# Three opening rounds of a fused Perceiver block re-made: earlier weight loads, Hadamard mean and absolute sums in round 0, ternary compares in round 1

## The reference

```python
# 1: cross attention, 16 heads, latent widths 64 (queries) and 32 (context)
C_q = Q @ Wq_d; C_kv = K @ Wkv_d
CqWqk = (C_q @ W_qk).reshape(b, n, H, LKV)
scores = einsum('bnhl,bkl->bhnk', CqWqk, C_kv) / sqrt(LKV)
out = einsum('bhnk,bkhd->bnhd', softmax(scores), (C_kv @ Wv_u).reshape(b, nkv, H, HD))
# 2: self attention, one head of width 128
q, k, v = split(x @ Wqkv + bqkv)
out = softmax(q @ k.T / sqrt(d)) @ v @ Wo + bo
# 3: feed forward with 4-bit activations and ternary weights
xh = x @ hadamard
scale = clip(max(abs(xh), axis=-1), 1e-5) / 7.0
xq = clip(round(xh / scale), -8, 7) * scale
wscale = clip(mean(abs(w), axis=1), 1e-5)
wq = where(w / wscale > 0.5, 1, where(w / wscale < -0.5, -1, 0)) * wscale
out = einsum('bsd,od->bso', xq, wq)
```

## Time and profile before

| | before |
|---|---|
| median of 3 runs (323.95 to 1033.37) | 324.0 us |
| profiled execution, its own time | 324.15 us |
| its span, first to last instruction | 322.4 us |
| PE busy (matmuls) | 310.4 us, 96% |
| DVE / ACT / POOL busy | 244.9 (76%) / 209.5 (65%) / 88.4 us (27%) |
| chain that ended last, by engine | PE 77%, DVE 10%, ACT 7% |
| DMA, mean over the span | 78 GB/s |

### The profile page before, as it was taken

How to read it: one execution, slowest core, us unless ns; L and a number is a source line. 1 busy time by engine, 2 the same in 40 slices (tenths; PEclk the granted TensorE clock), 3 DMA queues, 4 the chain that set the end, 5 groups by cost and what they waited for, 6 DMA issues and landing times.

```text
span 322.4 us, 8517 instructions
## 1 busy us (share of the span) xinstructions
PE 310.4 (96%) x3172; PEld 219.1 (68%) x3172; DVE 244.9 (76%) x524; ACT 209.5 (65%) x590; POOL 88.4 (27%) x129
## 2 busy tenths in 40 slices
PE   7987999999999999999999999999999999999995
PEld 6875776768576866667576867666675867675754
DVE  1499558887889878887889778987888877986435
ACT  1395867768596777767686777766776869582310
POOL 2000544041223324140323224240414123232320
PEclk9999999999999999999999999999999999999999
DMA  7891402050301403050302302050401010000000
GB/s 205 299 380 63 166 3 98 2 165 32 108 27 38 161 2 130 0 193 2 130 0 89 107 33 98 0 195 0 130 3 68 0 68 2 33 3 33 0 35 33
DMA packets 13481, 25.25 MB, mean 78 GB/s; under 512 B 3216, under 2 KB 3984, under 8 KB 13456
## 3 DMA queue, kind: packets, MB, share of 16 engines
q1 hardware_dynamic: 13456, 24.91, 22.4%
HBM read 20.71 MB, written 4.19 MB: 77 GB/s over the span
## 4 chain that ended last, share of the span: by engine, by line
PE 77%; DVE 10%; ACT 7%; issue 2%; DMA 1%; SPq 0%; POOL 0%; DVEq 0%
PE ps L691 12%; PE ps L729 8%; PE ps L638 7%; PE ps L806 6%; PE ps L786 5%; PE ps L648 4%; PE ps L829 4%; PE ps L838 4%; ACT prob L320 4%; PE ps L733 4%; DVE mx L450 3%; PE ps L709 2%; PE ps L741 2%; PE ps L669 2%; PE ps L812 2%
## 5 line engine op out<-in xcount | busy, mean ns | idle before, releaser
L320 ACT ACTIVATE prob<-ps,nmx,qk_scale 128x128 f32<-128x128 f32 x256 | 96.1, 468 | 40.5 <-DVE nmx L454 40.5
L691 PE MATMUL ps<-had_s,x3t 128*128 128x512 f32 x128 | 59.0, 604 | 1.1 <-ACT x3t L314 0.8
L450 DVE TENSOR_REDUCE mx<-ps 128x8 f32<-128x1024 f32 x32 | 38.9, 1216 | 11.1 <-PE ps L806 11.1
L691 PEld LDWEIGHTS ps<-had_s,x3t 128*128 128x128 f32 x128 | 23.0, 189 | 30.2 <-issue 28.4
L459 DVE TENSOR_REDUCE sum_a<-prob 128x8 f32<-128x1024 f32 x32 | 38.1, 1210 | 2.6 <-ACT prob L320 2.6
L303 POOL TENSOR_TENSOR qk_scale<-aux,power 128x1 f32<-128x1 f32 x16 | 8.8, 548 | 103.9 <-DVE aux L540 103.9
L314 ACT ACTIVATE prob_t<-ps 128x512 f32<-128x512 f32 x64 | 35.2, 622 | 0.6
L638 PE MATMUL ps<-ident,prob 128*128 128x128 f32 x256 | 33.7, 275 | 0.6 <-ACT prob L320 0.6
L729 PE MATMUL ps<-x2t,wqkv_s 128*128 128x128 f32 x256 | 32.7, 281 | 0.6 <-ACT x2t L314 0.2
L307 POOL TENSOR_TENSOR res<-prod,x 128x512 f32<-128x512 f32 x15 | 19.1, 1272 | 47.1 <-DVE prod L573 47.1
L729 PEld LDWEIGHTS ps<-x2t,wqkv_s 128*128 128x128 f32 x256 | 29.8, 191 | 2.6 <-ACT x2t L314 1.8
(11 more groups left out here) (120 smaller groups left out, 552.7 us busy)
## 6 DMA issues: line engine op xcount, KB each, us to landing
ct<-ctx_cols SPq DMA_DIRECT2D x16, 512.0 KB, 4.6
xt<-x_cols SPq DMA_DIRECT2D x16, 256.0 KB, 2.7
xr<-x_rows SPq DMA_DIRECT2D x16, 256.0 KB, 4.3
y<-res SPq DMA_DIRECT2D x15, 256.0 KB, 2.0
w_rows<-weight SPq DMA_DIRECT2D x1, 1024.0 KB, 8.8
had_s<-hadamard SPq DMA_DIRECT2D x1, 1024.0 KB, 9.0
wqkv_s<-wqkv SPq DMA_DIRECT2D x1, 768.0 KB, 10.6
wqk<-w_qk SPq DMA_DIRECT2D x2, 128.0 KB, 4.5
```

The costliest lines, as they stand in the source:

```text
L320: last = nc.scalar.activation(prob[:, h, :], ps[:, h // 4, (h % 4) * P:(h % 4) * P + P], ACT.Exp, bias=nmx[:, h:h + 1], scale=qk_scale[:])
L450: V.tensor_reduce(mx[:, h], ps[:, 2 * half:2 * half + 2, :].rearrange("p r (c k) -> p (r c) k", c=EC), AX.X, ALU.max).then_inc(done["mx"], 1)
L691: mm = pe.matmul(ps[:, B4, :], x3t[:, c, :], had_s[:, c, :], start=(c == 0), stop=(c == EC - 1))
```

## The change

Nothing of the arithmetic changes but the way in which the widened scales are turned (as transposes instead of matmuls with the identity). The orders of rounds 0, 1 and 2 do:
- SP: `had_s`, `w_rows` and the rows of pair 1 are loaded right behind the second context, `wqkv_s` behind the context of pair 2.
- Round 0: the latents are copied before the exponentials, DVE takes over three copies from ACT (`q_t`, `ckv`, the first quarter of `prob_t`), PE forms the Hadamard mean in two halves in bank B3 between the transposes, the scores of pair 1 come ahead of the weighted sum. DVE sums the absolute weights in four instructions, and then takes both halves of the largest scores. Of 14 filler matmuls 4 are left.
- Round 1: POOL centres the Hadamard matrix first (after the first half of `nmx` of pair 1), PE transposes all probabilities at once and then x2, DVE makes `const_row` and three ternary chunks, PE transposes the first half of the ternary weights (now by output rows, two chunks), and the scale row comes last.
- Round 2: the fourth ternary chunk on DVE behind `amax`, the second half of the ternary transposes in bank 0 (PE) and its copy (ACT).

```diff
@@ -211,21 +211,21 @@
             load_rows(0, 0)
             load_queries(1, 1)
             load_context(1, 1)
+            sp.dma_start(had_s[:], hadamard.rearrange("(c p) n -> p c n", p=P)).then_inc(ld_w["had"], 16)
+            sp.dma_start(w_rows[:], weight.rearrange("(c p) n -> p c n", p=P)).then_inc(ld_w["w"], 16)
+            load_rows(1, 1)
             for s in range(3):
                 sp.dma_start(b_qkv[:, s:s + 1], bqkv.rearrange("(s p o) -> s p o", p=P, o=1)[s]).then_inc(ld_w["b"], 16)
             sp.dma_start(bo_row[:], bo.rearrange("(o n) -> o n", o=1).to_broadcast([P, E])).then_inc(ld_w["b"], 16)
-            sp.dma_start(w_rows[:], weight.rearrange("(c p) n -> p c n", p=P)).then_inc(ld_w["w"], 16)
             sp.dma_start(wo_s[:], wo).then_inc(ld_w["wo"], 16)
             sp.wait_ge(zero_wv, 1)
             for r in range(4):
                 sp.dma_start(wv_bd[32 * r:32 * r + 32, :, 32 * r:32 * r + 32],
                              wv_u.rearrange("l (c r d) -> l c r d", c=EC, r=4)[:, :, r, :]).then_inc(ld_w["wv"], 16)
-            load_rows(1, 1)
-            sp.dma_start(had_s[:], hadamard.rearrange("(c p) n -> p c n", p=P)).then_inc(ld_w["had"], 16)
-            sp.dma_start(wqkv_s[:], wqkv.rearrange("(c p) n -> p c n", p=P)).then_inc(ld_w["wqkv"], 16)
             sp.wait_ge(made["lat"], 1)
             load_queries(2, 0)
             load_context(2, 0)
+            sp.dma_start(wqkv_s[:], wqkv.rearrange("(c p) n -> p c n", p=P)).then_inc(ld_w["wqkv"], 16)
...
             def hadamard_centred():
                 pool.wait_ge(hmean_read, 1)
+                pool.wait_ge(done["nmx"], 3)
                 for c in range(EC):
                     nc.gpsimd.tensor_tensor(had_s[:, c], had_s[:, c], had_mean[:], ALU.subtract).then_inc(had_ready, 1)
 
             def body(i, k, par, front, cross, self_, quant):
+                if isinstance(i, int) and i == 1:
+                    hadamard_centred()
...
+                def latents():
+                    after(act, made["lat"], i + 1)
+                    cols = slice(0 if alone(i) or par == 1 else P, P + 2 * SKV)
+                    copy(lat[:, cols], ps[:, B2, cols]).then_inc(read["lat"], 1)
+
+                def x2_turned():
+                    after(act, made["x2t"], i - 1)
+                    copy(x2t[:], ps[:, B2, :].rearrange("p (c t) -> p c t", c=EC)).then_inc(read["x2t"], 1)
+
+                def ternary_copy(half, bank):
+                    act.wait_ge(ternt_made, half + 1)
+                    copy(tern_t[:, :, 2 * half * P:2 * (half + 1) * P],
+                         ps[:, bank, :].bitcast(BF16).rearrange("p (c o) -> p c o", c=EC)).then_inc(ternt_read, 1)
+
+                if isinstance(i, int) and i == 0:
+                    latents()
                 if cross:
                     after(act, done["nmx"], i * 2)
                     exps(0, 6)
@@ -339,23 +356,24 @@
...
+                if isinstance(i, int) and i == 1:
+                    x2_turned()
+                    pt_copy(2)
+                    pt_copy(3)
+                    act.wait_ge(made["qt"], 3)
+                    q_copy(0, 0)
...
+                if isinstance(i, int) and i == 0:
+                    act.wait_ge(hmean_made, 1)
+                    copy(had_mean[:], ps[:, B3, :]).then_inc(hmean_read, 1)
...
+            def weight_sizes():
                 dve.wait_ge(ld_w["w"], 16)
-                V.tensor_reduce(w_abs[:], w_rows[:], AX.X, ALU.add, apply_absolute_value=True).then_inc(wabs_done, 1)
-                dve.wait_ge(wabs_done, 1)
+                for c in range(EC):
...
+                if first and i == 0:
+                    dve.wait_ge(made["qt"], 2)
+                    V.tensor_copy(q_t[:, 1], ps[:, B2, :].rearrange("p (c b q) -> p b c q", c=EC, b=2)).then_inc(read["qt"], 1)
+                    dve.wait_ge(made["ckv"], 2)
+                    V.tensor_copy(ckv[:, 1], ps[:, B1, 0:2 * SKV]).then_inc(read["ckv"], 1)
+                    sums(0)
+                    dve.wait_ge(made["pt"], 1)
+                    V.tensor_copy(prob_t[:, 0, :, :], ps[:, 0, :].rearrange("p (c t) -> p c t", c=EC)).then_inc(read["pt"], 1)
                     dve.wait_ge(ld_w["b"], 64)
                     V.tensor_copy(bv_wide[:], b_qkv[:, 2:3].to_broadcast([P, P])).then_inc(bvw_done, 1)
-                    ternary()
-                    dve.wait_ge(cb_made, 1)
-                    V.tensor_tensor(const_row[:], ps[:, B4, :], bo_row[:], ALU.add).then_inc(const_ready, 1)
+                    row_variance()
+                    dve.wait_ge(done["exp"], 2)
+                    row_scale()
+                    sums(1)
+                    weight_sizes()
+                    weight_scales()
+                    dve.wait_ge(made["s"], 2)
+                    largest(1, 0)
+                    largest(1, 1)
+                if first and i == 1:
+                    output_bias()
+                    dve.wait_ge(done["rsum"], 1)
+                    sums(0)
+                    ternary(0)
+                    sums(1)
+                    second_query()
+                    ternary(1)
+                    row_variance()
+                    row_scale()
+                    second_max()
+                    ternary(2)
...
+                    if first and i == 2:
+                        ternary(3)
...
-                pe.wait_ge(hmean_read, 1)
+                pe.wait_ge(ternt_read, 1)
                 for o in range(EC):
-                    mm = pe.matmul(ps[:, B4, o * P:(o + 1) * P], w_wide[:, o, :], ident[:], start=True, stop=True)
+                    mm = pe.transpose(ps[:, B4, o * P:(o + 1) * P], w_wide[:, o, :], ident[:])
                 mm.then_inc(row_made, 1)
 
-            def hadamard_mean():
...
+                for c in range(c0, c1):
+                    mm = pe.matmul(ps[:, B3, :], mean_w[:], had_s[:, c, :], start=(c == 0), stop=(c == EC - 1))
+                if c1 == EC:
+                    mm.then_inc(hmean_made, 1)
+
+            def ternary_transposed(half, bank):
+                pe.wait_ge(tern_done, 2 * (half + 1))
+                pe.wait_ge(const_ready, 1)
                 for c in range(EC):
-                    mm = pe.matmul(ps[:, B4, :], mean_w[:], had_s[:, c, :], start=(c == 0), stop=(c == EC - 1))
-                mm.then_inc(hmean_made, 1)
-
-            def ternary_transposed(half, bank):
-                pe.wait_ge(tern_done, EC)
-                if half == 0:
-                    pe.wait_ge(const_ready, 1)
...
-                        keep_busy(10, B3)
+                        keep_busy(4, B4)
+                        after(pe, read["lat"], i + 1)
+                        projected()
+                        hadamard_mean(0, 2)
                     transposed(0)
                     transposed(1)
                 if first and i == 0:
-                    after(pe, read["lat"], i + 1)
-                    projected()
-                    wide_bias()
+                    hadamard_mean(2, EC)
+                if first and i == 1:
+                    transposed(2)
+                    transposed(3)
+                    x2_turned()
+                    paired_projection()
...
+                if first and i == 2:
+                    pe.wait_ge(read["pt"], i * 4 + 1)
+                    ternary_transposed(1, 0)
+                if cross and not (first and i == 1):
                     transposed(2)
                     transposed(3)
                 if first and i == 0:
-                    keep_busy(4, B3)
-                if first and i == 1:
-                    wide_scale()
+                    wide_bias()
                 if self_:
...
+                if first and i == 0:
+                    scores()
+                if cross:
+                    weighted_sum()
+                if first and i == 1:
+                    ternary_transposed(0, B4)
+                if self_:
+                    after(pe, done["exp2"], i - 1, 2)
+                    pe.transpose(ps[:, B3, 0:P], p2[:], ident[:]).then_inc(made["p2t"], 1)
+                if front and not (first and i == 0):
+                    scores()
                 if self_:
...
-                if first and i == 0:
-                    ternary_transposed(0, B4)
-                    ternary_transposed(1, B3)
+                if first and i == 1:
+                    wide_scale()
```

179 lines of the change are left out of this document (93 added, 86 removed).

## The result

| | before | after |
|---|---|---|
| median | 323.93 us (19 runs, 323.14 to 326.11) | 322.61 us (20 runs, 321.47 to 324.84) |
| profiled execution, its span | 322.4 us | 320.5 us |
| mean granted clock of the profiled execution | 0.999 | 0.993 |

The account below looks back on a forecast made before the run. The prediction took PE to bound the kernel, so gains in rounds 0 to 2 move the end equally. Its terms, -3.2 us up to round 2 and +0.6 us in round 2, gave -2.6 us: 321.4 us, range 320.5 to 323.0.

Parts of the forecast that it names:

- the likeliest case: Rounds 0 to 2: the reordering gains as summed, -2.6 us, for 321.0 to 321.9 us; chance 0.52.
- the second case: Contention or late wait: POOL and DVE lock-out in SBUF, or pair 3's queries 1 us late; 322.0 to 322.9 us, chance 0.22.
- All four signs of "wrong": Granted clock under 1.00 after 29; PE waiting on x2n; longer round-1 DVE/POOL rows; PE or DVE waiting on a load.
- The opening of round 1 and the exponentials: Round 1 opens at 26.3 instead of 28.83; exponentials of pair 1 start at 26.85, 3.3 us sooner.
- The new wait of 2.2 us ahead of the second transposes: Round 1: PE waits from 30.8 to 33.0 for the second half of the exponentials, where the Hadamard mean lay.
- -3.2 us up to round 2: Rounds 0 and 1: round 2 opens at 44.4 instead of 47.63, 3.2 us gained.
- +0.6 us in round 2: Round 2: 8 ternary transposes on PE (0.53 us) and copy tern_t on ACT (0.97 us) cost 0.6 us in all.
- The sum of -2.6 us: Whole kernel: -3.2 us up to round 2 plus 0.6 us in round 2, giving 321.4 us.
- Hidden loads, "with little to spare": Rounds 0 and 1: the reordered Hadamard, weight and pair 3 query loads land in time; PE wants those queries at 27.4.
- x2n with 0.5 us to spare: Round 1: x2n is ready at 33.4, and must be turned at 33.9.
- The ternary chunks "hidden by PE's projections": Round 1: two DVE chunks of 1.28 us each end at 37.5; PE turns them at about 40.5, so they are hidden.
- the rival "slower (0.04): the clock": Round 1: PE idleness from 29.0 to 33.0 drops the clock to 1.2 GHz, up to 332.8 us; chance 0.04.

Follow-up runs that it names:

- after_again: The changed kernel run again with no edit: 322.99 us, ratio 0.9968 to the kernel before, 12 runs.
- fill_both: The changed kernel plus filler matmuls in both gaps of round 1, 6 before the first transposes and 8 before the second: 322.11 us, ratio 0.993.
- fill_second: The changed kernel plus 8 filler matmuls before the second transposes of round 1, on three chips: 321.91, 321.51 and 321.50 us.
- fill_second_again: The changed kernel plus 8 filler matmuls before the second transposes of round 1, repeated as control on another chip: 321.51 us, ratio 0.9908.
- after_third: The changed kernel once more with no edit, on the third chip: 323.61 us, ratio 0.9969 to the kernel before.
- the two direct comparisons: The changed kernel with 8 fillers against it without, same chip: 321.91 against 322.99 us on the first, 321.50 against 323.61 us on the third.

## Why the prediction came out as it did

The range held the time, but the likeliest case (321.0 to 321.9) did not, and the second case (322.0 to 322.9), in which it lies, named another mechanism, contention or a late wait. That the range held is in part luck: it was made wide for that case, and the clock, which filled it, had been left out of it. All four signs of "wrong" in the prediction appeared: a granted clock of 0.50 (after), PE waiting for x2n (0.17 us in after_again), longer rows of POOL (5.40 instead of 4.96 us), and DVE waiting on a load (0.73 us in after). Point by point:

- **The opening of round 1 and the exponentials**: right. 26.44 and 27.01 against 26.3 and 26.85, in the execution with the same start as before.
- **The new wait of 2.2 us ahead of the second transposes**: right, 2.08 and 2.09 us.
- **-3.2 us up to round 2**: right. Rounds 0 and 1 of after_again are 30.31 us against 33.41, which is -3.1.
- **+0.6 us in round 2**: right, 17.53 against 16.80 is +0.73.
- **The sum of -2.6 us**: with these two -2.4, and with 0.2 us behind round 3 that I did not trace, -2.2. The medians of the changed kernel's runs at a clock above 0.995, and those of fill_both and fill_second, lie 2.1 to 2.9 us below the kernel before.
- **Hidden loads, "with little to spare"**: half right. The queries of pair 3 and the weights cost nothing. The load that cost something was one whose place I had not weighed, the biases, now issued behind two loads of 1 MB: `bo_row` landed 9.5 us after its issue, 6.5 before. It held DVE for 0.73 and 1.12 us in the two profiled executions with a quick start.
- **x2n with 0.5 us to spare**: wrong by a little. In fill_second_again `x2n` ends at 33.44 (32.49 + 0.95) and PE takes it at 33.49, 1.11 us behind the transposes instead of 0.93. The centring took 5.4 us instead of 4.96 and `x2n` 0.2 us more. The rule weighed there was right in kind, but most of the lock fell on POOL, and PE lost 0.17 us, just under the 0.2 to 1.5 that this rival gave.
- **The ternary chunks "hidden by PE's projections"**: right. In fill_second_again the second chunk is ready at 37.16 (36.41 + 0.75), and PE turned it at 39.94: 2.8 us of cover.

**The step that failed** is the rival "slower (0.04): the clock". Its mechanism, place and trigger were what happened: in the profile of after the clock fell at 32.7, behind the two gaps, in that of after_third at about 29.4, behind the first. Two things were wrong. Its chance: I set 1.75 us of idleness at 1.00 against two gaps of together 2.7 to 3.7 us with 0.9 us of work between them, and took the first as evidence on the second. In 34 of 44 runs the mean clock was low, and in two of the three profiles it fell in round 1. And its size: I let the low clock run to the end of round 1 (11.4 us of loss) or far enough to decide the sign, as if it were all or nothing. It lasted 3.4 us in the profile of after, and about 7 us in that of after_third, partly over idle time; the loss was 1.4 and 1.7 us. A case "the clock falls for a few microseconds: 321.4 + 1.5 = 322.9" was missing, and by the runs it was the likeliest. The sum had a term too few, then: the clock stood at nothing in it, and so, with less weight, did x2n (0.17 us) and the biases' load.

A second weakness is the base. The forecast was set against one profiled execution whose start was one of many. For a change of 2 us that is a noise of the same size; it did not decide here, since before's median and its profiled execution agreed (323.93 and 324.15 us).

## What to carry to other kernels

When a change takes work out of the bottleneck engine's idle time, ask what keeps its clock up there: the Hadamard mean in round 1 was work and at the same time cover, and once it was gone the two gaps cost more than their own length. Put filler work into a gap that can't be closed (8 matmuls, 1.95 us inside a gap of 2.1 us, delayed nothing and brought 1.1 and 2.1 us in the two direct comparisons). And cut executions of one program at rows that all of them have before subtracting; a difference of 2 us in span may be the start of the execution.

## What was not expected of the hardware

- The clock of TensorE did not fall the same way each time: gaps of 0.80 and 2.08 us with 0.9 us of work between them left it at 1.00 in one execution, 0.66 and 2.08 us took it to 0.50 in another. What decides between them is open.
- The pace of the first microseconds differs between executions. The second latents of the same code were issued at 12.08 to 15.68 us. Much of this is PE's own pace: the first latents' row took 0.64 us in the two quick ones and 1.08 in all others but one, and the projection behind it 1.13 us in after and 2.08 in after_again, where the same rows of later rounds take 0.64 and 1.06. That is the ratio of the low clock, though the granted clock of these windows is recorded as 1.00. Why one execution starts at full pace and the next does not is open.
- POOL and DVE excluded each other for whole instructions, also where the DVE instruction has one SBUF tensor as its input (`w_neg`, 0.48 us alone, 1.46 us behind `x2b`). What it costs depends on which operations meet: 0.06 us on the row of `x2`, 3.3 us on those of two ternary chunks.
